# Attention and expert layer on one core: VectorE's early pieces put in another order, two routing weights made on ScalarE

## What is computed

```python
qh = split_heads(layernorm(x), Wq); kh = split_heads(ctx, Wk); vh = split_heads(ctx, Wv)
scores = einsum('bhqd,bhkd->bhqk', qh, kh) / scale          # scale = dk ** -0.5
attn = softmax(where(mask, NEG_INF, scores))
x = x + (attn @ vh) @ Wo.T
logits = layernorm(x) @ router_w.T
topk_scores, topk_idx = top_k(logits + router_bias, 2)
combine[token, topk_idx] += softmax(topk_scores)
out = sum_k combine[:, k] * down_k(silu(gate_k(xn)) * up_k(xn)) + shared expert
x = x + out
```

## Time and profile before

| what | value |
|---|---|
| median of 3 runs | 192.21 us (191.91 to 194.24) |
| the profiled execution, its own time | 192.32 us |
| its span in the trace | 190.5 us |
| TensorE, weight loads, VectorE, ScalarE, GpSimd busy | 91%, 66%, 85%, 68%, 47% |

### The profile page before, as it was taken

One profiled execution on the slowest core, in us unless ns is written; L12 is line 12 of the kernel. 1 busy time (PEld: TensorE's weight loads), 2 busy tenths in 40 slices (PEclk: granted clock), 3 DMA queues, 4 the chain that ended last, 5 costly groups with the idle time before them and its releaser, 6 DMA issues.

```text
span 190.5 us, 4273 instructions
## 1 busy us (share of the span) xinstructions
PE 173.7 (91%) x1305; PEld 125.4 (66%) x1305; DVE 161.5 (85%) x505; ACT 129.8 (68%) x288; POOL 89.4 (47%) x146
## 2 busy tenths in 40 slices
PE   7888888879699999999899889999999999999962
PEld 7763555445556666666658566778887887887841
DVE  5577989999689998999994799987989798989981
ACT  3195897778569989999788855566555656565641
POOL 7059993595968888888778790500000000000000
PEclk9999999999889999999999999999999999999999
DMA  5999100000000000000000533232345235323301
GB/s 112 305 326 392 60 2 2 3 0 0 5 0 2 3 0 0 0 0 3 2 0 19 170 105 110 110 126 92 122 122 173 80 128 167 115 90 121 116 2 55
DMA packets 12128, 15.43 MB, mean 81 GB/s; under 512 B 1744, under 2 KB 6608, under 8 KB 11984
## 3 DMA queue, kind: packets, MB, share of 16 engines
q1 hardware_dynamic: 10800, 13.79, 22.1%
q10 hardware_dynamic: 1312, 1.46, 2.8%
HBM read 14.06 MB, written 1.18 MB: 80 GB/s over the span
## 4 chain that ended last, share of the span: by engine, by line
PE 53%; DVE 19%; POOL 7%; issue 7%; ACT 6%; DMA 4%; ACTq 1%; DVEq 0%; POOLq 0%
PE bank L1093 30%; PE bank L1040 8%; PE bank L1031 4%; DMA mhalf<-mask_half 4%; PE bank L1022 4%; DVE hid L905 4%; DVE smax L828 4%; DVE prob L849 3%; POOL k_blk L453 3%; ACT hid_hi L660 2%; PE bank L1011 2%; PE bank L1001 2%; POOL rstd L427 1%; DVE hid_lo L897 1%; PE bank L991 1%
## 5 line engine op out<-in xcount | busy, mean ns | idle before, releaser
L1040 PE MATMUL bank<-k_blk,q_blk 128*128 128x512 f32 x64 | 34.8, 629 | 1.1 <-POOL k_blk L453 0.9
L651 ACT ACTIVATE sig<-bank 128x512 f32<-128x512 f32 x36 | 21.5, 599 | 19.6 <-PE bank L1093 18.5
L453 POOL TENSOR_TENSOR k_blk<-k_all,consts_sb 128x512 f32<-128x512 f32 x32 | 33.1, 1056 | 0.0
L660 ACT CAST hid_hi<-hid 128x512 fp32r<-128x512 f32 (+1 forms) x37 | 22.4, 608 | 11.4 <-DVE hid L905 11.3
L1093 PE MATMUL bank<-xt_hi,w_hi 128*128 (+1 forms) x72 | 29.2, 406 | 0.2 <-ACT sig L651 0.2
L1093 PE MATMUL bank<-xt_hi,w_lo 128*128 (+1 forms) x72 | 28.3, 393 | 0.0
L1093 PE MATMUL bank<-xt_lo,w_hi 128*128 (+1 forms) x72 | 28.2, 392 | 0.0
L897 DVE TENSOR_TENSOR hid_lo<-hid,hid_hi 128x512 fp32r<-128x512 f32 (+1 forms) x37 | 25.1, 679 | 3.7 <-ACT hid_hi L660 3.3
L600 ACT ACTIVATE prob<-prob,exp_scale 128x512 f32<-128x512 f32 x32 | 23.8, 743 | 2.5 <-DVE prob L849 2.5
L888 DVE TENSOR_TENSOR hid_u<-sig,bank 128x512 f32<-128x512 f32 x32 | 21.8, 682 | 4.1 <-PE bank L1093 2.5
L828 DVE TENSOR_REDUCE smax<-bank 128x8 f32<-128x512 f32 x32 | 21.9, 684 | 2.8 <-PE bank L1040 2.8
(11 more groups left out here) (117 smaller groups left out, 333.7 us busy)
## 6 DMA issues: line engine op xcount, KB each, us to landing
cb<-comb_rows SPq DMA_DIRECT2D x64, 128.0 KB, 2.9
w_moe_sb<-w_moe SPq DMA_DIRECT2D x1, 1296.0 KB, 10.7
ctxt_sb<-ctx_t SPq DMA_DIRECT2D x4, 256.0 KB, 8.7
xt_sb<-x_t ACTq DMA_DIRECT2D x4, 256.0 KB, 7.7
x_sb<-x SPq DMA_DIRECT2D x4, 256.0 KB, 10.3
out<-x_sb SPq DMA_DIRECT2D x3, 256.0 KB, 3.1
w_moe_sb<-w_moe SPq DMA_DIRECT2D x1, 432.0 KB, 8.0
w_att_sb<-w_att SPq DMA_DIRECT2D x1, 264.0 KB, 4.7
```

Of the source, the lines that this page charges most:

```text
L453: last = nc.gpsimd.tensor_tensor(k_blk[p][:, g, :, :], k_all[:, bass.ds(t, 1), g, :].broadcast_to([P, HG, S]), hmask_sb.rearrange("p (h o) ...
L651: nc.scalar.activation(sig[r][:, :], gate_ps[r][:, :], ACT.Silu).then_inc(s_sig, 1)
L660: nc.scalar.copy(hid_hi[k][:, cols], hid[k][:, cols]).then_inc(s_hid_hi, 1)
L1040: nc.tensor.matmul(score_ps[g][:, :], q_blk[q][:, g, :, :].rearrange("p b s -> p (b s)"), k_blk[q][:, g, :, :].rearrange("p h s -> p (h s) ...
```

## The change

Three edits.

1. VectorE's pieces by group are moved: `norm1(1)` from the end of step -1 to ahead of it, `keys(2)` from step 0 to step -1, `norm1(2)` from step 1 to step 0, `keys(3)` from step 2 to step 1, `norm1(3)` from step 3 to step 2. Step 3 has none. No instruction is added or taken out by this.
2. GpSimd's `rstd1_of(2)` and `rstd1_of(3)` move from steps 2 and 3 to steps 1 and 2; `rstd1_of(1)` stays in step 0.
3. `weights_of_two` is taken from VectorE. ScalarE makes the two weights right after the tanh, by two Identity activations with scale -0.5 and 0.5 and a bias of 0.5, behind a wait for its own tanh. `combined` waits for the marks by a new semaphore as well.

```diff
@@ combined
             eng.wait_ge(s_w_top, half + 1)
+            eng.wait_ge(s_marked, half + 1)
@@ gpsimd step
-                    if isinstance(t, int) and t in (0, 2, TRAIL):
-                        rstd1_of(1 + (t + 1) // 2)
+                    if isinstance(t, int) and t < GROUPS - 1:
+                        rstd1_of(t + 1)
@@ scalar tanh_of
                 nc.scalar.activation(half_tanh[:, tiles], gap[:, tiles], ACT.Tanh, scale=0.5).then_inc(s_tanh, 1)
+                act.wait_ge(s_tanh, half + 1)
+                for k, sign in ((0, -0.5), (1, 0.5)):
+                    last = nc.scalar.activation(w_top[:, tiles, k], half_tanh[:, tiles], ACT.Identity, scale=sign,
+                                                bias=half_sb[:, 0:1])
+                last.then_inc(s_w_top, 1)
@@ vector
-                dve.wait_ge(s_tanh, half + 1)
-                for k, sign in ((0, -0.5), (1, 0.5)):
-                    last = nc.vector.tensor_scalar(w_top[:, tiles, k], half_tanh[:, tiles], sign, 0.5, ALU.mult, ALU.add)
-                last.then_inc(s_w_top, 1)
@@ vector step
                 if isinstance(t, int) and t == LEAD:
                     keys(1)
-                    norm1(1, 1)
-                if isinstance(t, int) and 0 <= t <= TRAIL:
-                    g = 2 + t // 2
-                    if t % 2 == 0:
-                        keys(g)
-                    else:
-                        norm1(g, g % 2)
+                    keys(2)
+                if isinstance(t, int) and t == 0:
+                    norm1(2, 0)
+                if isinstance(t, int) and t == 1:
+                    keys(3)
+                if isinstance(t, int) and t == 2:
+                    norm1(3, 1)
                 if isinstance(t, int) and t == TILES - 4:
                     experts_marked(0)
-                    weights_of_two(0)
@@ vector, ahead of step -1
             norm1(0, 0)
+            norm1(1, 1)
             peel(step, LEAD)
```

## The result

| what | before | after |
|---|---|---|
| median of 20 runs each | 191.87 us (190.25 to 194.24) | 190.12 us (188.95 to 191.38) |
| the profiled execution, its own time | 192.32 us | 190.56 us |
| its span in the trace | 190.5 us | 188.7 us |
| mean granted clock in it | 0.991 | 0.985 |

The ratio leaves out slow executions (here three of the 20 of before, over 193.1 us), so it is not the quotient of the two medians. The forecast was 189.5, the range 188.5 to 191.8.

What follows compares the result with a forecast made beforehand. The prediction took TensorE to bound the kernel from step 4 on, VectorE and then GpSimd before that. A gain of 2.5 us plus 0.35 for the weights gave 192.32 - 2.85 = 189.5 us, range 188.5 to 191.8.

Steps and rivals of the forecast that it cites:

- The lead: Ahead of step 0: `norm1(1)` now stands before `smax` of step -1, which starts 0.20 us late.
- rival C: Ahead of the first softmax: `norm1(1)` waits for group 1's late load; 194 us if it lands at 21; chance 0.04.
- `keys(2)` beside `k_blk`: Step -1: `keys(2)` priced like `keys(1)` at 2.89 us, so step 0's `smax` starts 0.76 us later.
- Steps 0 to 2 level: VectorE's swapped pieces give the loss back; step 0 level within 0.15 us, steps 1 and 2 +0.16 and -0.16.
- Rival B: Pieces beside `k_blk` wait for one more GpSimd instruction, 1.0 us; gain 1.5 + 0.35, 190.4 us; chance 0.15.
- The stall moves to step 3: Step 4's stall comes again in step 3: `xn` 3.83 us after `veps` of 40.06, at 43.9.
- Step 4 regular, `smax` of step 5 at 51.7: Step 4 takes 4.52 us, so step 5's `smax` comes at 51.7 instead of 54.25, a gain of 2.5 us.
- The two delays that followed one another: VectorE's delay in step 3 and GpSimd's in step 4 were to lie side by side.
- rival A: TensorE's clock falls to 0.50 in step 3, costing 1.39 us; gain 1.1 + 0.35, 190.8 us; chance 0.27.
- The weights: Steps 12 and 13: VectorE's two `w_top` move to ScalarE; net gain 0 to 0.56 us, taken as 0.35.
- the main sum: Whole kernel: 2.5 + 0.35 = 2.85 us off the profiled execution's 192.32, giving 189.5 us.
- the 0.07 for a time under 188.4: Whole kernel: chance of a time faster than 188.4 us, needing a cheaper `rstd1_of(3)` chain than the trace has.

Runs made afterwards that it cites:

- e2: Edits 1 and 2 alone (the order) on the kernel before, weights left on VectorE; 189.34 us, ratio 0.9895 to before.
- e3: The changed kernel with GpSimd's `rstd1_of(2)` and `rstd1_of(3)` back in steps 2 and 3; 189.0 us, ratio 0.9869 to before.
- e1: Edit 3 alone (the weights on ScalarE) on the kernel before; 192.38 us against 191.55, ratio 1.0044.
- e4: The changed kernel with all groups' statistics, and GpSimd's `rstd1_of` for them, ahead of the keys of groups 2 and 3; 187.98 us, ratio 0.9813 to before.
- e9: e4 with `weights_of_two` back on VectorE as before; 187.99 us, ratio 0.984 to before.
- e8: e4 with four one-column memsets added at the head of VectorE's program; 187.93 us, ratio 0.9836 to before.

## Why the prediction came out as it did

Step by step, by the prediction's own statements:

- **The lead**, 0.20: it was 0.23 (5.88 us from the first `key_mean` to `smax` of step -1, for 5.65 in before). The load of group 1 was there (`veps` of `norm1(1)` done at 18.07, without a wait for a transfer); rival C did not come.
- **`keys(2)` beside `k_blk`**, 2.89 us, loss 0.76: it took 23.44 to 26.48 = 3.04. The rows show both locks: `key_mean` lasts 0.86 for a tile of 128x8 until the first half of `k_blk` is over, and the copy, 0.74 when alone (at 12.42), takes 1.54 from 25.04, past the end of the second half at 25.99. From step -1 to step 0 it is 8.38 instead of 7.68 us, with the lead a loss of 0.93. The Trainium skill, SBUF — State Buffer, "Who interferes with whom", had the mechanism right, each waits for a whole instruction of the other, and 0.93 lies nearer to the 1.05 worked out by it than to my 0.76. I had taken the price from another piece with the same neighbour instead of working it out from where the two meet.
- **Steps 0 to 2 level**: from `smax` of step -1 to that of step 1 it is 12.40 us, forecast 12.28 to 12.41. `norm1(2)` was not held up. Rival B did not come with its 1.0 us; its other half, that a part of `keys(2)` waits for one more GpSimd instruction, did (the `key_mean` of 0.86), at the small price above.
- **The stall moves to step 3**, `xn` at 43.9: it stands at 43.92, with 2.25 us of waiting for `bias`. Its two parts are off, and cancel: the start was 0.30 late by chance, and the chain from `veps` to `xn` took 40.48 to 43.92 = 3.44 instead of 3.83 us.
- **Step 4 regular, `smax` of step 5 at 51.7**: 47.18 and 51.73, 4.55 us for the step; no wait for `bias` in step 4. A gain of 2.52, forecast 2.5. The two delays that followed one another did come to lie side by side, and e2 and e3 show that it is VectorE's order that gains. But e3 gains 0.16 us more with GpSimd's delay in two portions, so the picture describes after but is not needed for the gain. That VectorE has one piece less to do in steps -1 to 3 fits as well, and no run separates it.
- **The clock**, rival A: full in steps 3 to 5 of the profiled execution (every stretch of 1 us from 40 to 56 us is granted 1.00), though TensorE was busy for only 0.28, 0.49 and 0.53 us of the three stretches from 42 to 45, a gap of the make that rival A had. Three of after's 20 executions, at 0.989 and with spans of 189.3 to 189.5, 1.5 us over the best group, may be such falls; none of them was profiled, so this stays open.
- **The weights**, 0.35: this term was mis-sized. Step 12 gained 0.56 as the upper bound said, and TensorE has no wait for `att` in step 13. ScalarE's activations cost nothing on the path: `v_blk` starts 0.65 us after the tanh instead of 0.10, as late as the upper bound of the price had it, but the second `prob_t` only 2.27 instead of 2.22, since the waits for TensorE between them took it up, as the prediction argued. But 0.53 to 0.66 came back in the expert part (e1 against before, e4 against e9), nearly all of it as gaps, which no row of before could show, and which the prediction had priced at nothing with a look at engine times alone.
- **What was missing**: that TensorE's clock can fall at the end, 0.74 us in the profiled execution. In that of before it stood. Why after falls there in 10 of 20 executions and e3, so like it, in none of 6, stays open.
- **Its sums**: the rivals' 190.8 and 190.4 come from the median of 192.21; from the 192.32 of the main sum they are 190.9 and 190.5. The forecast's own terms give 189.1 to 190.0, not 188.9 to 190.1, and the 0.07 for a time under 188.4 has no room beside chances that already add to 1. None of this changes the reading; the measured 190.12 lies above the forecast's own interval as its terms give it, and inside the range.

In the profiled execution the gain was 192.32 - 190.56 = 1.76 us where the sum said 2.85. The 1.09 us between them are 0.35 for the weights and 0.74 for the end; the smaller errors, the late start and the cheaper chain among them, cancel. That 189.5 came as near as 0.6 us to the median is in part luck: the gain was forecast too large by 1.1 us against the medians (2.85 for 1.75), and the time that it was taken from lies 0.45 above the median of all, 191.87.

**That execution is the larger flaw.** 1.39 of the forecast's 2.5 us were the clock's. Of 53 executions of before that ran beside the experiments, 28 have a mean clock of 0.998 to 1.0 (median span 188.85), and 19 one of 0.977, 0.990 or 0.991, near the 0.991 of the profiled one (190.0 to 192.5). After's four with 0.998 or 0.999 have 187.7 to 187.9. So in executions at the full clock the change gains about 1.0 us (0.5%), near the 1.1 that the prediction itself had left beside the clock's part, and only against those with the fall 2.5. The profile of e1, also at 0.991, has the same long step 4 (7.04 us). The 19 were not profiled, so that their fall came in step 4 too is likely and not shown. The Trainium skill, TensorE: Matmul & The Clock Gate, "What's actually happening", has the clock's windows run on by themselves; these groups agree, since one and the same program falls into the gap or not from one execution to the next. The prediction used that for the kernel after (rival A) and took the fall in the kernel before as given.

## What to carry to other kernels

Find what is needed first by the slowest chain, and put that first: here the statistics of all groups ahead of keys that nobody waits for yet gave 1.3 us more than the change, with the same work. Waiting time ahead of the pipeline is a cheap place for such a piece: `norm1(1)` cost 0.23 us there for its 1.39. When a saving hangs on a low clock in the profiled execution, compare the mean clocks of the other executions before counting it; it may be in a third of them. And an edit of half a microsecond in one stage is judged by a table of stages over the whole span, not by its own stage: it may come back elsewhere.

## What the runs showed of the hardware

VectorE can stand for 0.35 to 0.4 us with its inputs there, and the place of such a gap depends on how many instructions stand ahead of it in its program: four more at the head moved it from the expert loop to the attention loop. In both loops it came at one place of the round, and was largest in the first round (0.35, then 0.11 and 0.11; 0.39, then 0.15). A wait that the trace puts down to a semaphore can hide such a gap; the end of the releaser beside the start of the waiter tells them apart (0.10 and 0.45 us). And TensorE's clock fell at three different places in three kernels of the same work, around 51 us in before, 107 us in e8 and 183 us in after, at a price of 1.2 to 1.4, 0.6 and 0.7 us.
